# A six-phase Perceiver block on one core: the first phase's prologue taken tile by tile, with its mask, latent values and phase 2's weights moved

## The chip, the cores and the metric

The kernel runs on one core of a Trainium2 chip. The metric is the device time of one execution in microseconds (us); less is better. Times below are of the profiled execution where they carry a place in the trace (us from its start), and of three unprofiled runs where they are called the median.

## What is computed

The reference runs six blocks over x, 64 batches of 32 latent rows with 256 channels (2,048 rows, 16 tiles of 128), with a context of 64 x 257 rows of 192 channels and a mask over the context. The change touches the first block and the entrance of the second:

```
# block 1: cross-attention, 4 heads of 64, per batch
ln   = layernorm(layernorm(x)) * g + b            # 32 latent rows
cn   = layernorm(context) * g + b                 # 257 context rows
q    = rmsnorm(ln @ Wq)
k, v = concat(cn @ Wkv, ln @ Wlkv)                # 257 + 32 keys and values
k    = rmsnorm(k)
x    = x + softmax(masked(q k^T)) v @ Wo + bo     # mask on the 257 context keys
# block 2: self-attention within the 32 rows, 16 heads (16 for q, k and 64 for v)
x    = x + attend(layernorm(x)) @ Wout
# blocks 3 to 6: expert lookup, second cross-attention, state-space scan, routed experts
```

## The kernel before

`layers` (L2719) keeps the rows X in SBUF, 16 tiles of 128 x 256 floats, loads them in four quarters and calls the six phases one behind the other, with a barrier between them. Within a phase every engine has its own program, written by hand, and engines hand over through semaphores. There is no planner; the order of the code is the order of each engine. The helper `skewed(eng, n, depth, step)` (L244) lays a software pipeline over n items: at position v an engine treats item v, item v - 1 and so on, each at its own lag, the first six or so positions unrolled, the middle in a loop of two, the rest unrolled. U = 2 is the number of buffers of most tiles.

Phase 1 has three parts.

**Prologue (`phase1`, L278 to L551).** SP (the DMA queue's engine) issues the loads in order: the last context row of each batch, its vectors, wkv, then wq, wlkv, later weights, and the mask, broadcast to 128 partitions by one DMA (L365). DVE takes the statistics of all 16 tiles of X (L110, L113), normalises all of them into `lat` (L506), takes the statistics of `lat`, and normalises again tile by tile into `ln` (L532). GpSimd (POOL) raises variances to the power -0.5 (L386, L396). Ahead of the tiles stand small steps: PE multiplies the bias and the column sums of the context weights (L405, L408), DVE corrects `wc` (L514, L516), and the 257th context row of all 64 batches is normalised, projected (L417) and turned into the key column 0 of KE and the value row 0 of V3 (L421, L463, L367). Then a pipeline of 16 tiles: PE transposes `ln` (L432), ACT copies it scaled (L471), PE projects q, k and v (L438, L440), ACT squares q and k and copies v to `vl` (L476 to L479), DVE sums and scales (L539 to L547), PE transposes q and k (L446), DVE writes QT (L551) and ACT writes KE (L484). SP copies every `vl` in four DMAs, one a batch, into V3 in SBUF (L373). At the end ACT turns the whole mask from 'keep' to 'drop' (L489).

**Attention (`phase1_attention`, L561 to L776).** A pipeline over 64 batches with depth 4: SP loads two forms of the batch's context, rows (L610) and transposed (L612); DVE takes the rows' statistics (L765); PE multiplies keys and values (L677, L690), DVE scales them (L740), PE transposes keys (L684), forms scores (L657), DVE masks them (L747), ACT takes the exponential (L710), PE transposes the shares (L697) and multiplies them with the values (L669). For the 33 latent and last-row values ACT copies V3 into a double buffer `v3` (L712), which PE reads as its third operand.

**Output projection (`project_out`, L118).** PE multiplies tile by tile (L136). DVE first adds the bias bo to all of X (L148), then per tile adds the product (L154) and takes the statistics (L157).

Phase 2 (L783 on) loads its weights w and wo and the head mask itself (L838); its PE, POOL and DVE programs wait for all three. DVE aggregates, POOL raises to the power (L846), DVE sums the head masks (L1015) and normalises the first tile (L1049), PE transposes it (L961).

## Time and profile before

| what | value |
|---|---|
| median of 3 runs | 3019.74 us (3013.08 to 3022.22) |
| the profiled execution | 3020.78 us, its span 3018.9 us |
| PE busy | 2578.7 us, 85% of the span |
| DVE, ACT, POOL busy | 2065.5, 1479.5 and 619.0 us |
| DMA | 126.09 MB, mean 42 GB/s |
| phase 1 and the entrance of phase 2 | 0 to 560 us of the span |

The span runs from the first to the last instruction; the profiled execution's own time is 1.9 us longer. A row of the timeline gives start, length, engine, line, operation, the tiles written and read, the number of merged instructions, and in brackets the idle time before it with what ended it. "Idle before" of an engine that isn't the last to arrive costs nothing. A float32 matmul of the program stands as two records.

### The profile page before, as it was taken

The numbers are of one execution on the slowest core, as the hardware profiler recorded it, in microseconds if no ns is written. First come the engines' busy times: TensorE is split into PE (matmuls) and PEld (weight loads), VectorE is DVE, ScalarE is ACT, GpSimd is POOL, SyncE is SP. The second block draws the span as 40 slices with busy tenths as digits, with TensorE's granted clock in tenths as the row PEclk, the third lists the DMA queues.
The fourth block names the chain that finished last, engine by engine and source line by source line (L and its number), as shares of the span: only waits on it lengthen the run. The fifth ranks groups of instructions, "written<-read, shape, count | busy, mean of one in ns | idle before, by whom it ended". The sixth has DMA issues, their size and how long they took to land. (4 is left out here: it accounts for less than half of the span.)

```text
span 3018.9 us, 79963 instructions
## 1 busy us (share of the span) xinstructions
PE 2578.7 (85%) x29948; PEld 1912.8 (63%) x29949; DVE 2065.5 (68%) x4874; ACT 1479.5 (49%) x4043; POOL 619.0 (21%) x809
## 2 busy tenths in 40 slices
PE   6699999799788999999979999958467777779993
PEld 3488887455567888888855666633233333669992
DVE  6488887577539888888846888855589999532222
ACT  3555554255215555555526888812576864013330
POOL 3355554111000000000002222200222221012224
PEclk8799999899879999999989999979699999779996
DMA  3122221000300000000001111112000001441113
GB/s 95 46 68 63 65 65 40 36 1 0 139 37 2 2 3 2 2 2 2 2 21 46 45 46 49 39 40 105 0 1 1 1 1 56 161 182 36 37 35 94
DMA packets 71164, 126.09 MB, mean 42 GB/s; under 512 B 10176, under 2 KB 51392, under 8 KB 66368
## 3 DMA queue, kind: packets, MB, share of 16 engines
q1 hardware_dynamic: 67568, 114.06, 11.5%
q0 software_dynamic: 3408, 9.31, 1.1%
q8 instruction: 144, 2.36, 0.3%
q14 instruction: 44, 0.36, 0.0%
HBM read 103.48 MB, written 17.69 MB: 40 GB/s over the span
## 5 line engine op out<-in xcount | busy, mean ns | idle before, releaser
L1323 PE MATMUL s_ps<-s3e_xT,s_down 128*128 128x128 f32 x2048 | 256.0, 279 | 1.3 <-issue 1.3
L1323 PEld LDWEIGHTS s_ps<-s3e_xT,s_down 128*128 128x128 f32 x2048 | 244.9, 194 | 15.7 <-issue 10.2
L1334 PE MATMUL s_ps<-s_up,s3e_gh 128*128 128x256 f32 x1024 | 241.9, 380 | 3.6 <-DVE s3e_gh L1492 2.2
L1334 PEld LDWEIGHTS s_ps<-s_up,s3e_gh 128*128 128x128 f32 x1024 | 185.3, 190 | 25.9 <-issue 2.8
L1382 ACT ACTIVATE s3e_gh<-s_ps 128x512 f32<-128x512 f32 x128 | 76.5, 598 | 235.2 <-PE s_ps L1334 211.2
L2643 ACT ACTIVATE s6e_hT<-s_ps,s_b 128x128 f32<-128x128 f32 x312 | 84.7, 382 | 187.4 <-PE s_ps L2616 187.4
L2284 DVE SCALAR_TENSOR_TENSOR s5c_fresh<-s_ps,s5c_state 128x1024 f32<-128x1024 f32 x124 | 151.4, 1221 | 11.7 <-PE s_ps L2238 4.9
L1368 ACT ACTIVATE s3e_apart<-s3e_number,s3e_picksT 128x128 f32<-128x128 f32 x512 | 156.1, 388 | 1.6
L1688 PE MATMUL s_ps<-s4a_wv,s4b_cT 128*128 128x256 f32 (+1 forms) x512 | 152.8, 407 | 4.5 <-DMA s4b_cT<-ctxR 4.5
L2667 DVE TENSOR_TENSOR s6e_y<-s_ps,s_b 128x256 f32<-128x256 f32 x39 | 16.6, 425 | 202.2 <-PE s_ps L2630 202.2
L2616 PEld LDWEIGHTS s_ps<-s6e_xT,s6e_w 128*128 128x128 f32 x1248 | 147.1, 194 | 5.4 <-ACT s6e_xT L2647 3.5
L2616 PE MATMUL s_ps<-s6e_xT,s6e_w 128*128 128x128 f32 x1248 | 147.6, 277 | 2.9 <-ACT s6e_xT L2647 2.9
L677 PE MATMUL p_ps<-s_wc,s1b_cT 96*128 96x256 f32 x512 | 128.3, 394 | 19.8 <-DMA s1b_cT<-ctxT 19.8
L1691 PE MATMUL s_ps<-s4b_cT,s4a_wk 128*128 128x257 f32 (+1 forms) x512 | 144.6, 412 | 0.0
L2630 PE MATMUL s_ps<-s_w,s6e_hT 128*128 x624 | 141.2, 379 | 0.8 <-DVE s6e_y L2667 0.8
L2290 DVE TENSOR_TENSOR s5c_fresh<-s5c_fresh,s_ps 128x2048 f32<-128x2048 f32 x62 | 141.2, 2277 | 0.0
L1742 ACT ACTIVATE s4b_pr<-s4b_sc,s4b_nm 128x257 f32<-128x257 f32 x256 | 127.7, 502 | 27.3 <-DVE s4b_nm L1791 26.9
L192 POOL MEMSET s4q_half<- 128x1 f32 x1 | 0.1, 98 | 676.9 <-POOLq L2738 676.9
L2089 ACT ACTIVATE s5c_decay<-s5b_dt,s_rate 128x128 f32<-128x128 f32 x384 | 113.8, 388 | 46.1 <-PE s_ps L2238 44.3
L1295 PEld LDWEIGHTS s_ps<-s3e_col_hot,s3e_row_hot 128*32 128x32 f32 x8192 | 117.5, 110 | 27.6 <-issue 27.4
L1295 PE MATMUL s_ps<-s3e_col_hot,s3e_row_hot 128*32 128x64 f32 x8192 | 127.9, 220 | 0.8 <-issue 0.5
L2630 PEld LDWEIGHTS s_ps<-s_w,s6e_hT 128*128 128x128 f32 x624 | 115.5, 190 | 15.3 <-issue 1.2
(428 smaller groups left out, 6309.9 us busy)
## 6 DMA issues: line engine op xcount, KB each, us to landing
s4b_cT<-ctxR SPq DMA_DIRECT2D x64, 257.0 KB, 2.6
s_w<-p_w SPq DMA_DIRECT2D x16, 1024.0 KB, 13.0
s1b_cx<-ctx SPq DMA_DIRECT2D x64, 192.0 KB, 2.7
s1b_cT<-ctxT SPq DMA_DIRECT2D x64, 192.0 KB, 2.9
s_results<-s6e_y SPq DMA_DIRECT2D x39, 128.0 KB
s_down<-p_down SPq DMA_DIRECT2D x1, 4096.0 KB, 22.8
s_up<-p_up SPq DMA_DIRECT2D x1, 4096.0 KB, 32.0
s_silu_z<-s5p_sz SPq DMA_DIRECT2D x4, 1024.0 KB, 5.0
```

The lines of the kernel that those rows point to most:

```text
L677: mm = pe.matmul(banks[:, K_BANK + c.u, j * D:(j + 1) * D], lhsT=cT[:, c.u, k, tok(j)], rhs=wc[:, k, 0:D], start=k == 0, stop=k == 1)
L1295: mm = pe.matmul(banks[cs, bank, at:at + M], lhsT=row_hot[:, i % 2, j, cs], rhs=col_hot[:, i % 2, j, :], start=True, stop=True)
L1323: mm = pe.matmul(banks[:, H_BANK + i % 2, tok(e)], lhsT=down[:, k, i * CH + e, :], rhs=xT[:, c.u, k, :], start=k == 0, stop=k == KT - 1)
L1334: mm = pe.matmul(banks[:, Y_BANK, 0:D], lhsT=gh[:, o.u, e, :], rhs=up[:, e, :], start=e == 0, stop=e == NE - 1)
L1368: ins = act.activation(apart[:, j, :], number[:], ACT.Abs, bias=picksT[:, t.u, 0, q:q + 1], scale=-1.0)
L1688: return pe.matmul(banks[:, V_BANK, j * D:(j + 1) * D], lhsT=cT[rows, d.u, k, tok(j)], rhs=wv[rows, k, :], start=j == k, stop=j != k)
L1691: return pe.matmul(banks[:, K_BANK + m, 0:CTX], lhsT=wk[rows, k, tok(m)], rhs=cT[rows, d.u, k, :], start=k == 0, stop=k == 1)
L1742: ins = act.activation(pr[:, e.u, n, :], sc[:, e.u, n, :], ACT.Exp, bias=nm[:, e.u, n:n + 1], scale=-1.0, accum_out=sums[:, bass.ds(e.b, 1 ...
L2284: dve.scalar_tensor_tensor(part_of(fresh, h, part, 2), banks[:, D_BANK:D_BANK + 2, :].rearrange("p j d -> p (j d)"), floor, part_of(state, ...
L2290: dve.tensor_tensor(part_of(fresh, h, 0, HG), part_of(fresh, h, 0, HG), banks[:, I_BANK:I_BANK + HG, :].rearrange("p j d -> p (j d)"), ALU ...
L2616: mm = pe.matmul(banks[:, H_BANK + 2 * m.u + f // 4, tok(f % 4)], lhsT=w[:, m.u, k, tok(f)], rhs=xT[:, m.u, k, :], start=k == 0, stop=k == ...
L2630: mm = pe.matmul(banks[:, Y_BANK, 0:D], lhsT=hT[:, o.u, f, :], rhs=w2[:, bass.ds(e, 1), f, :], start=f == 0, stop=f == FT - 1)
```

## The change

- Only x's first quarter and the identity matrix are loaded ahead of phase 1; the other quarters are issued within it, between the weights, which are reordered: wq and wlkv come first.
- `skewed` takes a function `beside(v)`, called ahead of position v outside the loop. The small steps that stood ahead of the tiles are spread over the positions of the pipeline with it. `lat` and the second statistics are gone: the variance of both normalisations is formed at once from the first (`var * (1 + eps) + eps^2`), per quarter of x, and `ln` is read from X.
- POOL adds bo to each tile of X in the pipeline; the output projection gets no bias.
- The mask is loaded once (64 x 257 bytes), turned by ACT, stored to memory (`dropped`) and read back broadcast, four batches a tile.
- The latent values are stored per tile to memory (`v3d`) by one DMA; the last row's values by a DMA from ACT's queue. In the attention SP loads 33 rows per batch from there into `v3`; ACT's copy goes.
- The first two batches' context is loaded at the prologue's end, into buffers that now outlive it.
- Phase 2's w and wo are loaded in sixteenths beside the mask pieces, from a class `Second`.

Where the small steps go: on PE the bias row stands at position 3, the column sums at 4, the context row's transposes at 6, its projection at 16 and its key column at 20. On DVE the statistics of the four quarters stand at positions 0, 3, 4 and 5, the context weights and row statistics at 2, the row's normalisation at 3, the bias copy and the correction of `wc` at 5, the row's sums at 17 and its key at 19.

The core of the diff:

```diff
+def skewed(eng, n, depth, step, link=None, links=0, beside=None):
     def lone(v):
+        if beside:
+            beside(v)
         step(lambda s: Item(0, v - s) if 0 <= v - s < n else None)
...
             def _(sp):
-                for dst, src in ((cvec, "p1_cvec"), (wkv, "p1_wkv"), (vec, "p1_vec"), (wq, "p1_wq"), (wlkv, "p1_wlkv")):
-                    sp.dma_start(dst[:], I[src]).then_inc(load, 16)
-                sp.dma_start(mask8[:, :, 0:CTX], I["mask_BxS2_bk0"].unsqueeze(0).broadcast_to([P, B, CTX])).then_inc(load_late, 16)
-                sp.dma_start(V3[0:1, :, :], cv[:]).then_inc(cv_loaded, 16)
-                    for b in range(BT):
-                        sp.dma_start(V3[1:S + 1, c.b * BT + b, :], vl[b * S:b * S + S, c.u, :]).then_inc(v3_loaded[c.u], 16)
+                for dst, src in ((vec, "p1_vec"), (wq, "p1_wq"), (wlkv, "p1_wlkv")):
+                    sp.dma_start(dst[:], I[src]).then_inc(load_p, 16)
+                rows(1)
...
+                rows(2)
+                rows(3)
+                sp.dma_start(kept[:], I["mask_BxS2_bk0"]).then_inc(load_m, 16)
...
+                def beside(v):
+                    if v == 1:
+                        sp.wait_ge(mask_turned, 1)
+                        sp.dma_start(dropped, kept[:]).then_inc(mask_stored, 16)
+                        sp.wait_ge(mask_stored, 16)
+                        sp.wait_ge(mask_zeroed, 1)
+                    if v == NT:
+                        for c in (Item(0, 0), Item(0, 1)):
+                            load_context(sp, c)
+                            load_turned(sp, c)
                 def step(item):
+                    c, m = item(0), item(1)
+                    if c:
+                        sp.wait_ge(vl_ready, c.b + 1)
+                        sp.dma_start(v3d[bass.ts(c.b, BT), 1:S + 1, :], vl[:, c.u, :]).then_inc(v3_stored[c.u], 16)
+                    if m:
+                        sp.dma_start(mask8[:, bass.ts(m.b, BT), 0:CTX], dropped[bass.ts(m.b, BT), :].unsqueeze(0).broadcast_to([P, BT, CTX])).then_inc(mask_loaded, 16)
+                        g.second.load(sp, I, m.b)
...
             def _(pool):
+                def beside(v):
+                    if v == 0:
+                        deviations(0)
+                        pool.wait_ge(load_bo, 16)
+                    if v == 3:
+                        pool.wait_ge(cstat_ready, 1)
+                        pool.tensor_tensor(crs[:], cve[:], half[0:B, :], ALU.pow).then_inc(crstd_ready, 1)
+                        deviations(1)
...
+                        pool.wait_ge(ln_ready, c.b + 1)
+                        pool.tensor_tensor(X[:, c.b, :], X[:, c.b, :], bo[:], ALU.add)
...
             def _(act):
-                act.wait_ge(load_late, 16 * 4)
-                act.activation(mask8[:, :, 0:CTX], mask8[:, :, 0:CTX], ACT.Copy, bias=1.0, scale=-1.0)
+                    if v == 3:
+                        act.wait_ge(load_m, 16)
+                        act.activation(kept[:], kept[:], ACT.Copy, bias=1.0, scale=-1.0).then_inc(mask_turned, 1)
+                    if v == NT:
+                        act.dma_start(v3d[:, 0, :], cv[:]).then_inc(cv_stored, 16)
...
             def _(dve):
-                for t in range(NT):
-                    ins = dve.tensor_scalar(lat[:, t, :], X[:, t, :], mv[:, t, 0:1], rstd[:, t:t + 1], ALU.subtract, ALU.mult)
-                row_stats(dve, link, stats, mv, var, LN_EPS, lat).then_inc(stat_ready, 1)
+                def spread(i):
+                    dve.wait_ge(g.x_loaded[i], 16)
+                    for t in range(i * XC, (i + 1) * XC):
+                        last = dve.bn_stats(stats[:, t, :], X[:, t, :])
...
+                    dve.tensor_scalar(var[:, cs], mv[:, cs, 1], 1.0 + LN_EPS, LN_EPS * LN_EPS, ALU.mult, ALU.add).then_inc(stat_ready, 1)
...
-        project_out(nc, g, "s1o", banks, OT, wo, bo)
+        project_out(nc, g, "s1o", banks, OT, wo)
...
+                c, a = item(0), item(LAG_AT)
+                if a:
+                    after(sp, pv, a.b - 1)
+                    sp.dma_start(v3[0:S + 1, a.u, :], v3d[bass.ds(a.b, 1), :, :].rearrange("b s d -> (b s) d")).then_inc(v3_loaded[a.u], 16)
-                    pe.wait_ge(v3_ready, o.b + 1)
+                    pe.wait_ge(v3_loaded[o.u], 16 * (o.turn + 1))
-                    act.activation(v3[0:S + 1, a.u, :], V3[:, a.b, :], ACT.Copy).then_inc(v3_ready, 1)
...
-            for dst, src in ((w, "p2_w"), (wo, "p2_wo"), (headmask, "headmask8")):
-                sp.dma_start(dst[:], I[src]).then_inc(load, 16)
-            sp.wait_ge(load, 16 * NLOAD)
...
+    def load(self, sp, inputs, t):
+        cols = bass.ts(t, 1536 // NT)
+        sp.dma_start(self.w[:, :, cols], inputs["p2_w"][:, :, cols]).then_inc(self.loaded, 16)
+        sp.dma_start(self.wo[:].rearrange("p v (h d) -> p (v h) d", h=2)[:, bass.ds(t, 1), :],
+                     inputs["p2_wo"].rearrange("p v (h d) -> p (v h) d", h=2)[:, bass.ds(t, 1), :]).then_inc(self.loaded, 16)
```

## Rows read from the trace of the kernel before

**Rows 1.** Busy time by stretch: length, then each engine, granted clock, DMA share, GB/s
```profile
43.60:101.00 57.40, 51.33 (x200) 30.93 (x200) 37.85 (x106) 30.57 (x99) 24.61 (x15) 0.97 0.15 36
...
120.00:500.00 380.00, 377.86 (x4547) 304.93 (x4548) 305.31 (x924) 203.90 (x605) 210.17 (x309) 0.99 0.23 65
```

**Rows 2.** Timeline up to the first tile's second normalisation
```profile
3.53 3.96 POOL L382 MEMSET s_mask<- 128x4624 uint32 x1
...
5.46 4.02 DVE L110 BATCH_NORM_STATS2 p1a_stats<-x_rows 128x6 f32<-128x256 f32 x12 [5.31 <-DMA x_rows<-x]
...
11.34 1.17 DVE L113 BATCH_NORM_AGGREGATE p1a_mv<-p1a_stats 128x2 f32<-128x6 f32 x16
...
12.87 2.94 POOL L386 TENSOR_TENSOR p1a_rstd<-p1a_var,s_half 128x16 f32<-128x16 f32 x1 [5.38 <-DVE p1a_var L115]
...
21.84 1.28 ACT L455 ACT_TABLE_LOAD   x1 [21.68 <-PE p_ps L413]
...
32.37 0.72 DVE L532 TENSOR_SCALAR p1a_ln<-p1a_lat,p1a_mv,p1a_rstd 128x256 f32<-128x256 f32 x2
```

**Rows 3.** Timeline of PE and POOL in the tile pipeline, seventh to sixteenth tile
```profile
54.59 0.38 PE L432 MATMUL p_ps<-x_ident,p1a_ln 128*128 128x128 f32 x2
...
81.16 1.88 PE L440 MATMUL p_ps<-s_wlkv,p1a_lnT 128*128 128x512 f32 x4
...
87.18 0.41 PE L432 MATMUL p_ps<-x_ident,p1a_ln 128*128 128x128 f32 x2
...
77.71 1.63 POOL L396 TENSOR_TENSOR p1a_rn<-p1a_ss,s_half 128x8 f32<-128x8 f32 x1 [1.93 <-DVE p1a_ss L547]
```

**Rows 4.** Timeline of ACT at the prologue's end
```profile
94.56 0.39 ACT L479 ACTIVATE p1a_vl<-p_ps 128x256 f32<-128x256 f32 x1
...
101.39 0.62 ACT L484 ACTIVATE s_KE<-p_ps,s_vec 128x128 f32<-128x128 f32 x2 [1.98 <-DVE s_QT L551]
101.90 13.94 ACT L489 ACTIVATE s_mask<-s_mask 128x16448 uint8<-128x16448 uint8 x1
```

**Rows 5.** DMAs: V's issue durations (ns), L612's landing, the mask's size and landing (us)
```profile
L373 SPq DMA_DIRECT2D s_V<-p1a_vl x64: 527/530/837, 41.1 to 97.1; - x64
...
DMA to landing us min/median/max: 2.8/2.9/3.9
...
s_mask<-mask_BxS_bk SPq DMA_DIRECT2D x1, 2056.0 KB, 16.7
```

**Rows 6.** Timeline at the start of the attention block
```profile
116.10 0.31 POOL L617 MEMSET s1b_pT<- 128x256 f32 x1 [18.80 <-POOLq L314]
...
120.49 3.78 PE L677 MATMUL p_ps<-s_wc,s1b_cT 96*128 96x256 f32 x8 [19.84 <-DMA s1b_cT<-ctxT]
...
124.31 0.88 DVE L740 SCALAR_TENSOR_TENSOR s1b_kn<-p_ps,s1b_crs,s_bias 128x256 f32<-128x256 f32 x2 [4.76 <-PE p_ps L677]
```

**Rows 7.** Attention: groups of ACT and POOL (120 to 510 us), timeline of SP and PE
```profile
L712 ACT ACTIVATE s1b_v<-s_V 33x256 f32 (+1 forms) x62 | 24.8, 400 | 0.0
...
L629 POOL TENSOR_TENSOR s1b_qb<-s_QT,s_headmask 128x256 f32<-128x256 f32 x63 | 38.8, 615 | 60.1 <-DVE s1b_kn L751 60.1
...
132.40 0.59 SPq L612 DMA_DIRECT2D s1b_cT<-ctxT  x1
...
139.76 0.25 PE L669 MATMUL p_ps<-s1b_pT,s1b_v 128*32 128x32 f32 x8
```

**Rows 8.** Output projection: timeline of DVE and PE, and one stretch as in rows 1
```profile
522.12 4.42 DVE L148 TENSOR_TENSOR x_rows<-x_rows,s_bo 128x4096 f32<-128x4096 f32 x1 [3.33 <-PEq L571]
...
522.12 16.49 PE L136 MATMUL p_ps<-s_wo,s_OT 128*128 128x256 f32 x64 [0.60 <-PEq L571]
...
524.00:526.00 2.00, 2.00 (x6) 1.64 (x5) 2.00 (x1) 0.00 (x0) 0.00 (x0) 0.50 0.00 0
```

**Rows 9.** Timeline at the start of phase 2
```profile
542.47 2.90 POOL L846 TENSOR_TENSOR s_rstd<-s_var,s_half 128x16 f32<-128x16 f32 x1 [1.47 <-DVE s_var L115]
...
550.30 0.16 DVE L1015 TENSOR_REDUCE s_fourmask<-s_headmask 128x4 f32<-128x8 f32 x1 [7.98 <-DMA s_headmask<-headmask]
```

More of the change, by code:

```diff
@@ L253, in skewed @@
         lone(v)
+    if beside and lead != lead + 2 * ((n - lead) // 2):
+        beside(lead)
     trips = (n - lead) // 2
@@ L263, in skewed @@
         lone(v)
+    if beside:
+        beside(n + depth)
 def straight(n, depth, step):
@@ L316, in sa @@
                 return actx.enter_context(nc.sbuf_tensor("p1a_" + name, shape, dt))
+            wq = sa("wq", [P, KT, D])
+            wlkv = sa("wlkv", [P, KT, 2 * D])
+            wkv = sa("wkv", [DH, 2, 2 * D])
+            cvec = sa("cvec", [DH, 2, 2])
+            bo = sa("bo", [P, D])
+            kept = sa("kept", [B, CTX], U8)
             stats = sa("stats", [P, NT, 6])
@@ L321, in phase1 @@
             rstd = sa("rstd", [P, NT])
-            lat = sa("lat", [P, NT, D])
             ln = sa("ln", [P, U, D])
@@ new lines, in _ @@
+                g.second.start(sp, I)
+                def beside(v):
[8 more added lines that the diff above has]
+                            load_turned(sp, c)
@@ L379, in _ @@
+                skewed(sp, NT, 2, step, beside=beside)
+                sp.wait_ge(cv_stored, 16)
+                for q in v3_stored:
+                    sp.wait_ge(q, 16 * NT // U)
+                sp.wait_ge(mask_loaded, 16 * NT)
+                sp.wait_ge(load_late, 16 * 2)
             @block.gpsimd
@@ L390, in _, with step @@
+                def step(item):
+                    c = item(2)
+                    if c:
+                        pool.wait_ge(ss_ready, c.b + 1)
+                        pool.tensor_tensor(rn[:, c.u, :], ss[:, c.u, :], bc(half[:], P, 8), ALU.pow).then_inc(rn_ready, 1)
+                        pool.wait_ge(ln_ready, c.b + 1)
+                        pool.tensor_tensor(X[:, c.b, :], X[:, c.b, :], bo[:], ALU.add)
+                skewed(pool, NT, 4, step, beside=beside)
                 pool.wait_ge(css_ready, 1)
@@ L447, in step @@
                         mm.then_inc(qk_tr, 1)
-                skewed(pe, NT, 4, step)
+                skewed(pe, NT, 4, step, beside=beside)
             @block.scalar
             def _(act):
-                act.wait_ge(load, 16 * NLOAD)
-                act.wait_ge(c_tr, 1)
-                for k in range(2):
-                    ins = act.activation(cT[:, k, :], ps[0:DH, 0, 0, k * B:(k + 1) * B], ACT.Identity,
-                                         bias=cvec[:, 1, k:k + 1], scale=cvec[:, 0, k:k + 1])
@@ L606, in _ @@
         def _(sp):
+            sp.wait_ge(zeroed, 2)
             def step(item):
-                c = item(0)
-                after(sp, cmv_ready, c.b - 1)
-                sp.dma_start(cx[:, c.u, :, :], I["ctx_768"][c.b, 0:2 * P, :].rearrange("(j p) c -> p j c", p=P)).then_inc(cx_loaded[c.u], 16)
-                after(sp, values, c.b - 1)
-                sp.dma_start(cT[:, c.u, :, :], I["ctxT"][c.b, :, :, 0:2 * P]).then_inc(c_loaded[c.u], 16)
-            skewed(sp, B, 0, step)
+                c, a = item(0), item(LAG_AT)
+                if c and not (isinstance(c.b, int) and c.b < U):
+                    after(sp, cmv_ready, c.b - 1)
+                    v["load_context"](sp, c)
+                    after(sp, values, c.b - 1)
+                    v["load_turned"](sp, c)
+                if a:
+                    after(sp, pv, a.b - 1)
+                    sp.dma_start(v3[0:S + 1, a.u, :], v3d[bass.ds(a.b, 1), :, :].rearrange("b s d -> (b s) d")).then_inc(v3_loaded[a.u], 16)
+            skewed(sp, B, 3, step)
         @block.gpsimd
@@ L794, in phase2 @@
         banks = s.psum()
-        w = sb("w", [P, KT, QKV])
-        wo = sb("wo", [P, VT, D])
-        headmask = sb("headmask", [P, HK])
+        w, wo, headmask, load = g.second.w, g.second.wo, g.second.headmask, g.second.loaded
         fourmask = sb("fourmask", [P, R4])
@@ L2738, in layers @@
             nc.all_engine_barrier()
+        with ExitStack() as ahead:
+            g.second = Second(Scope(nc, ahead, "s2w"))
+            for phase in (phase1, phase2):
+                run(phase)
+        for phase in (phase3, phase4, phase5, phase6):
+            run(phase)
 def layout(a):
```

264 lines of the change are left out of this document (151 added, 113 removed).

## The prediction

> **What bounds the kernel now.** I read the stage windows first, then the timeline of each engine through the first 135 us, the waits, and then the two places after the attention loop that the diff touches. From 120 to 500 us TensorE (PE) is busy 377.86 of 380.00 us at a granted clock of 0.99: the attention loop is PE-bound and nothing taken from ScalarE (ACT) or VectorE (DVE) shortens it [rows 1]. What can be gained lies before and after it. Before it, the prologue has four serial stretches: statistics and a full normalisation of all 16 tiles up to 32.37 us, in which PE only works on small things [rows 2]; the tiles, 3.6 us each, at which PE is busy 51.33 of 57.40 us [rows 1, 3]; the mask turned by one ACT instruction of 13.94 us with nothing beside it [rows 4]; and the start of the attention block at 116.10, whose first transposed context is used at 120.49 [rows 6]. After it come the bias add of 4.42 us and the wait for phase 2's weights [rows 8, 9].
>
> **First tile earlier.** Only the first quarter of x is issued before the first barrier, three issues fewer, so phase 1's block begins at about 3.1 instead of 3.5. The first quarter is used at 5.46 now [rows 2]; I keep 5.4. Its statistics: 4 x 0.335 (4.02 / 12), 4 x 0.07 for the aggregates (16 of them take 1.17), 0.2 for the variance, and three hand-overs of some 0.05: 2.0, so 7.4. POOL's clearing of the mask (3.96 us from the block's start) ends then too. The power over 16 columns takes 2.94 and over 8 columns 1.63 [rows 2, 3], 0.16 a column, so 1.0 for 4: 8.4. The first normalised tile starts at about 8.9 instead of 32.37, 23.5 earlier. The pass into `lat` and the second statistics go; they are inside this 23.5. The weights wq and wlkv stand in the queue behind 0.6 MB instead of 2.6 MB and come at 7 to 8, by my reading no wait.
>
> **What the fill gives back.** Between the first tile and step 7 of the pipeline the old kernel needed 22.2 us (32.37 to 54.59, the seventh tile's transposes) [rows 2, 3]. The new one has three more things there. ACT's table load, 1.28 [rows 2], now sits between the first transposes and the second, since both use one bank: 1.3. PE gets two pairs of 512-column products (bias row and column sums), 1.88 a pair as in the tile loop [rows 3]: 3.8. DVE gets 9.9: context weights 0.9, context row 0.7, three spreads of statistics at 2.0, 0.4, bias copy and weight correction 2.0. Walking the steps in order, PE is busy with cold first projections and the extra products until about 31, and DVE's normalisation of the sixth tile ends at about 33, behind QT, bias, correction and last spread: 2.3 of the 9.9 show. Together 7.4, of which some 1.4 falls in gaps that the old fill had. Given back: 6.0. Bounds: nothing of DVE's work shows (gives back 3.7), or all does (15). I take the walk, since DVE idled over half of the old fill. Net shift at step 7: 17.5.
>
> **The tiles.** From 54.59 to 87.18 nine steps take 32.6, 3.62 each, PE-bound [rows 3]; I leave them. POOL gets x + bo per tile. The nearest row is qb, 128 x 256 from two SBUF inputs, 0.615 [rows 7]; beside its 1.63 it makes 2.25 of 3.62, behind the power it shall not delay. Price zero, covered by POOL's idle 2.0 per step; if the cover were gone it would add to rn, on which DVE waits. SP has four issues a step as now: one latent store for four, and one mask piece and two weight pieces. Now each takes 0.53 to 0.84 [rows 5], with some 0.15 between, so 2.7 a step. The new ones have more dimensions; at 0.6 to 0.7 each they take 2.9 of 3.62: covered. The latent store is used again two steps (7.2 us) later; landings are 2.9 (a batch of transposed context) to 16.7 (the whole mask of 2 MB, which shares the engines with the other loads) [rows 5], a sixteenth of it much less. Before them SP waits for the turned mask (64 x 257 bytes: about 0.4 on ACT), stores it and waits for it, some 3 us after ACT's step 3, when the second tile's values aren't yet there: zero.
>
> **The tail.** The context row's projection on PE in step 16 costs 1.9. The row's key column costs 0.6 behind the last KE, which ended at 102.01 [rows 4]. So ACT ends at 102.0 - 17.5 + 1.9 + 0.6 = 87.0; square sums and powers of that row lie in DVE's drain idle of 2 us. SP: the last value is copied at 94.95 - 17.5 + 1.9 = 79.4 [rows 4]; behind it come a store, three pieces, four context loads, three pieces: 11 issues at 0.6 = 86.0, landing 2.9 later, 88.9. SP is last. The 13.94 of the mask is gone, with the 0.26 of the barrier kept: the attention block starts at 89.1 instead of 116.10. **27.0 gained.**
>
> **First context.** Now from block start to the first kn is 8.2 us (116.10 to 124.31), because loads are issued inside the block. With both tiles loaded, PE starts keys at once, cold, 3.78 [rows 6], and DVE's statistics with POOL's power (about 2.1) lie beside: 4.0. **4.2 gained**; at full clock the keys would take 1.9, the other bound is 6.1.
>
> **Attention loop.** ACT loses the V copy, 62 x 0.400 = 24.8 [rows 7]. The cover is PE: worth zero, apart from a few tenths in the drain. SP gets a third DMA per item: V for item 0 would be issued behind the transposed context at 133.0 and is used at 139.76 [rows 7], 6.7 us of slack against a landing of 2.9 [rows 5]. Zero, and decided by that slack.
>
> **Output projection.** The 4.42 add on DVE looks like a gain and is none: PE starts at the same 522.12 at clock 0.50 until past 526, DVE catches up, and PE ends the stage: 16.49 busy, without gaps [rows 8]. Between 0 and 4.4; I take 0, since what ends the stage is PE's last product at 538.6 with one add and one statistic behind it.
>
> **Phase 2.** DVE waits 7.98 us for the masks, until 550.30; the power, which would then be last, ended at 545.37 [rows 9]. With everything there, DVE goes on at 545.4. **4.9 gained.** The clock after it is cold either way.
>
> **Sum.** 27.0 + 4.2 + 4.9 = 36.1. The profiled execution took 3020.78 us (span 3018.9), 1.04 above the median of 3019.74. 3020.78 - 36.1 = 2984.7; I say 2984.
>
> **Two rules against it.** The piecewise loads: the rows show four issues per step fitting in 2.7 to 2.9 of 3.62. The Trainium skill, "DMA: Bandwidth & Descriptors", section on rules for kernel authors, says to coalesce small transfers, which below 64 KB are mostly overhead; these are 64 to 128 KB, and by it the queue would set the pace. With the rows the sum has nothing for it, by the rule it has rival B's 5 us; no row of before shows such a piece.
> The add on POOL: no row has a two-input POOL operation beside DVE's normalisation. The Trainium skill, "SBUF — State Buffer", section "SBUF: two separate sides", says that DVE and GpSimd share one port pair as an exclusive lock, held for a whole instruction, where DVE runs a 2-port mode or reads two SBUF tensors; here DVE's operations read one tensor, at 0.405 for 256 columns, so by it they'd pass, and the sum stays. Were the lock taken all the same, it is rival C, priced from rows.
>
> **Rivals.**
> A. The fill is serial: most of DVE's 9.9 shows (7.6 more). For: DVE is in order, and its spreads stand ahead of the normalisation that PE waits for. Against: its idle there. Gain 28.5, time 2992; chance 0.15.
> B. SP sets the tile's pace. At its longest issue (0.84 + 0.15, four a step = 3.96) 14 steps lose 5: gain 31, 2990. Chance 0.07. It would also need the latent store to hold back ACT.
> C. POOL's add blocks DVE or delays rn: 16 x 0.62 = 9.9: gain 26, 2995. Chance 0.05.
> D. The bias add was on the path: 4.4 more, 2980. Chance 0.06.
> E. Slower: V from memory comes late in the attention loop. Place: PE's V product of each item; price: landing less 6.7 us, times 64. At a landing of 7.1 the gain falls below 9 us, at 7.4 the kernel is slower by over 0.3%; 8 us would cost 83 and give 3068. Against: no context landing is over 3.9. Chance 0.03 slower, 0.03 about equal.
> F. A part doesn't do what it says: phase 2 or the first context still waits for something not seen (the clearing of a buffer, a weight piece last in the queue). 4 to 5 less, 2989. Chance 0.05.
> The forecast itself, gains of 31 to 41: 0.56.
>
> **The numbers.** A difference of 0.3% (9 us) is about what a measurement of this kernel can tell from no change. The range reaches to A and C on one side, with the runs' own spread (3013 to 3022), and on the other takes in full clock at the first keys (1.9), D (4.4) and a fill without DVE (2.3): 2972 to 2997. Faster 0.93, within 0.3% 0.04, slower 0.03.
>
> **What the profile after would show.** First `ln` near 9 us; seventh tile's transposes near 37; steps of 3.6; no 13.9 us ACT row; attention's memsets near 89, with the keys at once and first kn 4 us later; the same 6.0 us per item; output projection still 16.5 us of PE; no DMA wait at the start of phase 2. Wrong would be: steps over 3.7 us with SP never waiting (B) or rn late (C), PE idle over 3 us around steps 4 to 6 (A), a wait of PE for V in attention (E), attention starting more than 3 us from 89.

## The result, and the profile after

The changed kernel takes 2987.71 us (median of 4 runs, 2986.72 to 2989.41), the kernel before beside it 3020.82 (4 runs, 3013.08 to 3022.22): a ratio of 0.9896, 95% interval 0.9878 to 0.9914. The profiled execution took 2988.56 us, its span 2986.7. Span against span the gain is 32.2 us, where the prediction's sum said 36.1. A later profiled execution of the same kernel, beside edit 9, stood at 773.03 at the start of phase 3, where this one stood at 772.93, and had a span of 2984.2: behind that place two executions of one program differ by 2.6 us.

The two stretches of [rows 1], the windows of the changed kernel:

```profile
43.60:101.00 57.40, 45.42 (x171) 27.02 (x169) 32.14 (x96) 24.66 (x79) 30.96 (x32) 0.91 0.53 115
120.00:500.00 380.00, 373.60 (x4620) 300.67 (x4619) 301.47 (x907) 187.26 (x552) 203.46 (x300) 0.99 0.24 65
```

At the same clock times these cover other work: the first now holds the end of the tiles and the start of the attention, the second ends behind the attention. So the places have to be followed one by one. First the fill, which answers to [rows 2, 3], from the timelines of POOL, DVE and PE:

```profile
3.22 3.96 POOL L421 MEMSET s_mask<- 128x4624 uint32 x1
5.13 1.41 DVE L569 BATCH_NORM_STATS2 p1a_stats<-x_rows 128x6 f32<-128x256 f32 x4 [4.99 <-DMA x_rows<-x]
7.48 1.05 POOL L427 TENSOR_TENSOR p1a_rstd<-p1a_var,s_half 128x4 f32<-128x4 f32 x1 [0.30 <-DVE p1a_var L574]
8.56 0.73 DVE L620 TENSOR_SCALAR p1a_ln<-x_rows,p1a_mv,p1a_rstd 128x256 f32<-128x256 f32 x2 [1.36 <-POOL p1a_rstd L427]
```
```profile
28.89 1.88 PE L501 MATMUL p_ps<-p1a_wlkv,p1a_lnT 128*128 128x512 f32 x4
...
33.30 0.43 PE L493 MATMUL p_ps<-x_ident,p1a_ln 128*128 128x128 f32 x2 [1.84 <-DVE p1a_ln L620]
33.88 1.69 PE L499 MATMUL p_ps<-p1a_wq,p1a_lnT 128*128 128x256 f32 x4
35.35 3.06 PE L501 MATMUL p_ps<-p1a_wlkv,p1a_lnT 128*128 128x512 f32 x4
...
38.69 0.38 PE L493 MATMUL p_ps<-x_ident,p1a_ln 128*128 128x128 f32 x2
...
73.64 0.44 PE L493 MATMUL p_ps<-x_ident,p1a_ln 128*128 128x128 f32 x2
```

The first tile starts at 8.56 instead of 32.37. PE waits 1.84 for the sixth tile's normalisation, and the product behind that gap takes 3.06 where the one before it took 1.88 (the granted clock is 0.57 from 34 to 38 us). The seventh tile's transposes stand at 38.69, the sixteenth's at 73.64, with the context row's 1.93 between.

The tail and the attention's start, which answer to [rows 4 to 6], from the timelines of ACT, SP, POOL, PE and DVE:

```profile
80.26 0.39 ACT L550 ACTIVATE p1a_vl<-p_ps 128x256 f32<-128x256 f32 x1
...
87.28 0.62 ACT L555 ACTIVATE s_KE<-p_ps,s_vec 128x128 f32<-128x128 f32 x2 [1.95 <-DVE s_QT L639]
87.80 0.58 ACT L535 ACTIVATE s_KE<-p_ps,s_vec 128x64 f32<-128x64 f32 x2
```
```profile
80.84 0.60 SPq L407 DMA_DIRECT2D s_v<-p1a_vl  x1
81.64 0.41 SPq L409 DMA_DIRECT2D s_mask<-s_dropped  x1
...
83.75 0.40 SPq L317 DMA_DIRECT2D s_bcx<-ctx  x1
...
86.22 0.60 SPq L409 DMA_DIRECT2D s_mask<-s_dropped  x1
86.86 0.61 SPq L2814 DMA_DIRECT2D s2w_w<-p_w  x1
87.52 0.60 SPq L2815 DMA_DIRECT2D s2w_wo<-p_wo  x1
```
SP's waits between 80 and 93 us:
```profile
SPq L415 <- DMA s_mask<-s_dropped: 3.0, 1, 3.0
```
```profile
92.06 0.31 POOL L709 MEMSET s1b_pT<- 128x256 f32 x1 [7.10 <-POOLq L322]
...
92.10 3.75 PE L769 MATMUL p_ps<-s_wc,s_bcT 96*128 96x256 f32 x8 [5.15 <-PEq L322]
...
95.89 0.88 DVE L830 SCALAR_TENSOR_TENSOR s1b_kn<-p_ps,s1b_crs,s_bias 128x256 f32<-128x256 f32 x2 [2.88 <-PE p_ps L769]
```

The 13.94 of the mask is gone. ACT is done at 88.38. SP issues until 88.12 and then waits 3.0 for the last mask piece, issued at 86.22 and landed 4.9 later, so SP ends the stage. The two weight pieces behind it are waited for only in phase 2. The keys start 0.04 behind the block.

Behind the attention, which answers to [rows 8, 9], from the timelines of PE, POOL and DVE:

```profile
492.83 16.86 PE L136 MATMUL p_ps<-s_wo,s_OT 128*128 128x256 f32 x64 [0.58 <-PEq L660]
...
513.60 2.89 POOL L928 TENSOR_TENSOR s_rstd<-s_var,s_half 128x16 f32<-128x16 f32 x1 [1.47 <-DVE s_var L115]
...
516.53 0.16 DVE L1097 TENSOR_REDUCE s_fourmask<-s2w_headmask 128x4 f32<-128x8 f32 x1 [3.08 <-POOL s_rstd L928]
```

DVE waited 7.98 for a DMA there; it now waits 3.08 for the power. Where the time went, from the starts of the same instructions (us; the last column is the running gain):

| place | before | after | gain so far |
|---|---|---|---|
| first `ln` | 32.37 | 8.56 | 23.8 |
| seventh tile's transposes | 54.59 | 38.69 | 15.9 |
| sixteenth tile's transposes | 87.18 | 73.64 | 13.5 |
| attention block | 116.10 | 92.06 | 24.0 |
| first `kn` | 124.31 | 95.89 | 28.4 |
| output projection | 522.12 | 492.83 | 29.3 |
| DVE's head-mask sum in phase 2 | 550.30 | 516.53 | 33.8 |
| start of phase 3 | 804.30 | 772.93 | 31.4 |
| span | 3018.9 | 2986.7 | 32.2 |

### The profile page after: what moved, and what is told of

The parts are those of the page before. It is cut to its first block and busy times, and to the rows that moved or that the text cites. A ratio compares the mean times of both kernels' runs of the same rounds, so it can differ in the third digit from the quotient of the medians.

```text
span 2986.7 us, 80073 instructions
## 1 busy us (share of the span) xinstructions
PE 2578.9 (86%) x29948; PEld 1912.3 (64%) x29949; DVE 2050.2 (69%) x4827; ACT 1447.7 (48%) x3979; POOL 628.6 (21%) x827
## 5 line engine op out<-in xcount | busy, mean ns | idle before, releaser
L2749 DVE TENSOR_TENSOR s6e_y<-s_ps,s_b 128x256 f32<-128x256 f32 x39 | 16.6, 424 | 200.8 <-PE s_ps L2712 200.8
L769 PE MATMUL p_ps<-s_wc,s_bcT 96*128 96x256 f32 x512 | 128.1, 394 | 5.2 <-PEq L322 5.2
```

What stands on the lines that cost most here:

```text
L769: mm = pe.matmul(banks[:, K_BANK + c.u, j * D:(j + 1) * D], lhsT=cT[:, c.u, k, tok(j)], rhs=wc[:, k, 0:D], start=k == 0, stop=k == 1)
```

## The experiments

Eleven variants ran, and the changed kernel once more. Where a single time stands the kernel ran once, and it is compared with the profiled changed kernel by its places in the trace; where there were several runs, medians and intervals stand. The totals of single runs decide little: in edits 4 and 8 the seventh tile starts 2.6 and 2.8 us earlier than after the change, in code that those edits leave alone (see the fill, below).

**1. The bias add alone.** The kernel before, with `bo` left out (the output then lacks it):

```diff
-        project_out(nc, g, "s1o", banks, OT, wo, bo)
+        project_out(nc, g, "s1o", banks, OT, wo)
```

> The kernel before, with the add of bo to X left out of the output projection. If PE ends that stage, the stretch from its first product to the next phase's aggregates (522.12 to 540.94 before) keeps its 18.8 us within 0.5 and the kernel its time. If the bias add was on the path, it shrinks by 4.4 us.

Measured 3017.59 us beside 3022.39. PE's 64 products took 15.54 instead of 16.49 and started at 520.81; from their start to DVE's aggregates in phase 2 there were 17.87 us instead of 18.82. The 0.95 between the two is PE's own duration, that is the clock; behind the change itself the same stretch is 19.24, with the add gone. The 4.42 us row was hidden, and rival D falls. The total alone would have pointed the other way, 4.8 below the run beside it; but runs of the kernel before range from 3013.08 to 3024.2, and at the start of phase 3 the two stand at 804.23 and 804.30.

**2. The context loads back inside the attention.** The loads at position 16 go, the attention's SP issues them; its wait for the cleared buffers moves behind them, to the first load of V.

```diff
@@ prologue, sync
-                    if v == NT:
-                        for c in (Item(0, 0), Item(0, 1)):
-                            load_context(sp, c)
-                            load_turned(sp, c)
@@ attention, sync
-                if c and not (isinstance(c.b, int) and c.b < U):
+                if c:
```

> The kernel after, with the first two batches' context loaded inside the attention block again. The first kn comes 8.2 us after the block's start instead of 3.8 (+4.4). But SP has four issues fewer at the prologue's end: if SP's queue is what ends the prologue, the block starts 2 us earlier than 92.06, and the first kn stands at 98.3, net +2.4. If ACT ends the prologue, the block's start stays and the net is +4.4.

Measured 2989.05. From block to first `kn` 8.04 us instead of 3.83, as expected (before 8.2). But the block came at 88.85, 0.26 behind ACT's last write of KE, 3.2 us earlier than after the change. The net is 1.0 later at the first `kn` (96.89), 0.5 later than in the changed kernel's other profile (96.38). So the four issues ahead of the last mask piece in SP's queue cost 3.2 of the 4.2 that they bring, and they hold the end of the prologue. By the total, 2989.05 against 2985.78 to 2989.41 of the changed kernel, the early loads are worth nothing that can be told.

**3. Phase 2's weights loaded whole in phase 2, as before the change.**

```diff
-                        g.second.load(sp, I, m.b)
+            for dst, src in ((w, "p2_w"), (wo, "p2_wo")):
+                sp.dma_start(dst[:], I[src]).then_inc(load, 16)
```

> The kernel after, with w and wo of phase 2 loaded in phase 2 again, one DMA each. First normalisation of phase 2 moves from 4.5 to about 9.4 us behind the phase's first aggregate (+4.8). SP issues two DMAs fewer per tile: if SP ends the prologue, the attention block starts 2 to 2.5 us earlier than 92.06, net +2.5; steps of the tile pipeline stay 3.65 us if neither SP nor the small rows cost anything there, and fall to 3.61 if they did.

Measured 2990.32. The tiles' step stayed at 3.67 us (34.96 from the seventh to the sixteenth tile, less the context row's 1.93, over nine steps), without the two weight pieces a step as with them (before 3.62), which removes rival B: the pieces cost the tiles nothing. The block came at 89.98, 2.1 earlier. Only 0.9 of that is SP's shorter tail (from ACT's last KE to the block 2.76 instead of 3.68); the other 1.2 stood already at the sixteenth tile (72.46 instead of 73.64). The last mask piece was issued 2.5 earlier, at 83.74, but SP waited 5.1 for it. The wait came back, in DVE's timeline:

```profile
517.07 0.16 DVE L1101 TENSOR_REDUCE s_fourmask<-s2w_headmask 128x4 f32<-128x8 f32 x1 [7.55 <-DMA s2w_wo<-p_wo]
```

4.5 lost at phase 2's entrance, 0.9 gained in the tail.

**4. The mask turned whole at the end again**, by the long ACT instruction.

```diff
-                        act.activation(kept[:], kept[:], ACT.Copy, bias=1.0, scale=-1.0).then_inc(mask_turned, 1)
+                        act.activation(kept[:], kept[:], ACT.Copy).then_inc(mask_turned, 1)
...
+                act.wait_ge(mask_loaded, 16 * NT)
+                act.activation(mask8[:, :, 0:CTX], mask8[:, :, 0:CTX], ACT.Copy, bias=1.0, scale=-1.0)
```

> The kernel after, with the mask stored unturned and turned in the 128-partition copy at the prologue's end, as in the kernel before. The turning needs the last piece, which lands at about 91, so it stands fully behind SP: attention starts at 92.06 + 13.9 = 106 us. If the pieces' landing were not what ends the prologue, ACT would turn from 88.4 on and attention start at 102.6 (+10.5).

Measured 2996.61. The timeline of ACT:

```profile
85.24 0.58 ACT L535 ACTIVATE s_KE<-p_ps,s_vec 128x64 f32<-128x64 f32 x2
88.21 13.95 ACT L560 ACTIVATE s_mask<-s_mask 128x16448 uint8<-128x16448 uint8 x1 [2.40 <-DMA s_mask<-s_dropped]
```

From ACT's last KE to the block there are 16.6 us instead of 3.7: 12.9 for 13.95 of instruction, since ACT had idled there behind SP. It is the largest single part of the gain behind the fill. The block's place, 102.42, looks like the second figure of the expectation (102.6, if the landing didn't count); it isn't that case, since the trace shows ACT waiting 2.40 for the last piece. ACT's last KE simply ended 2.6 earlier, at 85.82. For the same reason the total rose by 8.9 only.

**5. DVE's small work out of the fill.** The bias copy goes to ACT at position 4, the correction of `wc` to DVE's position 16.

```diff
@@ vector
-                    if v == 5:
-                        dve.tensor_copy(bias[:], banks[:, B_BANK, :]).then_inc(bias_ready, 1)
+                    if v == NT:
                         for k in range(2):
                             ins = dve.scalar_tensor_tensor(wc[:, k, :], ...)
@@ scalar
+                    if v == 4:
+                        act.activation(bias[:], banks[:, B_BANK, :], ACT.Copy).then_inc(bias_ready, 1)
```

> The kernel after, with DVE's correction of wc moved from position 5 to 16 and the bias copy given to ACT at position 4. DVE reaches the sixth tile 2 us earlier, so PE's wait of 1.84 us at 31.5 goes. If that wait is also what let the clock fall (the next products took 3.06 instead of 1.88 and 1.69 instead of 1.03), the seventh tile's transposes move from 38.69 to about 35.0 (3.6 to 3.7 gained). If the wait alone counts: 36.8.

Measured 3005.28, 17.6 us slower than the change. The first half went as expected: PE's 1.84 gap was gone, the granted clock from 34 to 38 us was 1.00 (0.57 after the change), and the seventh tile's transposes stood at 35.31 instead of 38.69. Here the wait and the slow products behind it went together: from the fifth tile's transposes to the seventh's 8.27 us instead of 11.49, that is 3.2, of which the gap is 1.8 and the clock 1.4. Edits 4 and 8 show that they aren't one cost: there the same gap stood at the same place, 1.83, the products behind it took 1.13 and 1.88, and from the sixth tile to the seventh there were 3.97 and 3.98 us instead of 5.39. Then two losses that no theory had. PE at position 16 needs `wc` before DVE, a position behind, has corrected it (timeline of PE; first row with the wait, whose products are slow again):

```profile
71.71 3.65 PE L479 MATMUL p_ps<-p1a_wkv,p1a_cT 96*64 96x512 f32 x4 [3.26 <-DVE s_wc L606]
75.28 0.69 PE L493 MATMUL p_ps<-x_ident,p1a_ln 128*128 128x128 f32 x2
```

5.0 lost. And phase 3, which this kernel entered 1.1 us ahead of the changed one (771.83 against 772.93), was longer by 17.0 us from its normalisation at 876.3 (876.9 after the change) to the last one (541.9 instead of 524.9), in code that the edit doesn't touch. DVE's waits there, 1080 to 1400 us (waiter, what it waited for, us in total, times, longest), and PE's from 1050 to 1500:

```profile
DVE s3e_xn L170 <- issue: 16.7, 4, 4.3
```
```profile
PE s_ps L1396 <- DVE s3e_xn L170: 8.9, 4, 2.4
```

"Issue" is time in which DVE waited for nothing that the profile shows. In the changed kernel it has none in this loop.

**6. SP's tail shortened.** The whole mask by one DMA at position 1, phase 2's weights in four parts within the attention, the context loads at position 4.

```diff
+                        sp.dma_start(mask8[:, :, 0:CTX], dropped.unsqueeze(0).broadcast_to([P, B, CTX])).then_inc(mask_loaded, 16)
-                    if v == NT:
+                    if v == 4:
                         for c in (Item(0, 0), Item(0, 1)):
...
-                    if m:
-                        sp.dma_start(mask8[:, bass.ts(m.b, BT), 0:CTX], ...)
-                        g.second.load(sp, I, m.b)
@@ attention, sync
+                if 2 <= v < 6:
+                    g.second.load(sp, I, v - 2)
```

> The kernel after, with the mask read back in one DMA once it is stored, the first context loads issued at position 4, and phase 2's weights loaded in quarters at the start of the attention. SP's last issue in the prologue is the last latent store (80.8, landed by 85), so ACT's last write at 88.4 ends it: attention starts at 88.7 instead of 92.06, 3.4 gained. If something else than SP's queue held it, the start stays at 92. The weights cost the attention nothing if a transposed context still lands within its 6 us of slack; otherwise PE waits for it in the first steps.

Measured 2982.73. ACT's last KE ends at 88.71 and the block starts at 88.97: SP no longer ends the stage, 3.1 us gained at the first `kn` (92.80), and 2.9 of it still there at the start of phase 3.

**7. V from memory loaded one position later**, where it is used at once.

```diff
-                c, a = item(0), item(LAG_AT)
+                c, a = item(0), item(LAG_OUT)
...
-            skewed(sp, B, 3, step)
+            skewed(sp, B, 4, step)
```

> The kernel after, with each batch's V rows loaded one step later, so that the slack of 6.6 us is gone (about 0.6 us left). PE then waits for V in every item: landing of 2.5 to 3 us less 0.6, so 2 to 3 us for each of 64 items, 130 to 190 us in all. If the loop hid it (V not on PE's path) the time would stay.

Measured 3172.59, 184 us more, 2.9 an item. PE's waits between 100 and 600 us, and that kernel's window against [rows 1]:

```profile
PE p_ps L761 <- DMA s1b_v<-s_v: 104.5, 53, 2.3
```
```profile
120.00:500.00 380.00, 297.51 (x3138) 236.28 (x3137) 206.28 (x621) 131.43 (x374) 141.69 (x208) 0.88 0.18 47
```

Each item waits up to 2.3, and PE's clock falls with the gaps (0.88 granted). Rival E's place is right, and what keeps it away is the one position of slack. Its price is too low: by its formula an item costs what it waits, 2.3 at most, and here it cost 2.9, the rest being products at the lower clock.

**8. ACT's copy kept**, as a dummy copy of as many elements per item in the attention.

> The kernel after, with a copy of 33 x 256 values put back into ACT's step of the attention where the V copy stood (to a buffer nobody reads). 64 x 0.4 = 25.6 us of ACT's busy time come back. If PE bounds the loop, an item stays at 6.07 us and the time is the same within 1 us; if ACT's order counted, up to 25 us more.

Measured 2986.02. The groups of ACT in that attention:

```profile
L804 ACT ACTIVATE s1b_spare<-s_bias 33x256 f32<-33x256 f32 x63 | 25.2, 400 | 0.0
```

25.2 us of work came back. The total, 2.5 below the profiled changed kernel's, isn't the proof of that, since the first `kn` stood 2.8 earlier, at 93.07, by the clock in the fill. The stage is: from first `kn` to the output projection 397.8 us before, 396.9 after the change, 397.8 here. The 24.8 of the old copy were worth at most 0.9, and less than can be told: without the copy the same stretch took from 396.1 (edit 11) to 398.2 (edit 9).

**9 and 10. Fill and tail together, beside the changed kernel itself.** The correction of `wc` at DVE's position 6, the bias copy left where it is, and the whole of edit 6; and the changed kernel unaltered.

```diff
@@ vector, from position 5 to position 6
+                    if v == 6:
+                        dve.wait_ge(rstd_ready, 4)
                         for k in range(2):
                             ins = dve.scalar_tensor_tensor(wc[:, k, :], ...)
```

> Moves DVE's correction of wc (two of 0.63 us) from position 5 of the tiles to position 6, where DVE had 1.0 us of idle time, and makes the whole of the change to SP's tail that the earlier kernel made (mask copied with one DMA, second phase's weights in four parts instead of 16, context loads at position 4). DVE issues as many instructions as in the changed kernel. My theory (the DVE-caused PE gap of 1.84 us and the cold clock behind it are one cost of 3.4 us; SP's tail is another of 3.1 us, and they add): PE's wait for ln(5) falls to about 0.6 us, its next products run at 1.88 us or at most half of the 1.2 us excess stays, T(6) at 35.9 to 36.5, the block at 86.0 to 86.8 by ACT, span 2978 to 2980, a ratio to the kernel before of 0.986 to 0.988. Rival (the DVE work only moves its wait to position 6 and costs there what it saved): T(6) at 38 or more or T(7) - T(6) at 5, total as with the tail alone, 2983. Rival (a loss in the third phase, as when DVE lost one instruction): +17 us there, total 2996.

> The changed kernel unaltered, as the measure for the run beside it: 2987 to 2990 us, ratio 0.989 to 0.990 to the kernel before. In its third phase DVE waits for no instruction (issue idle 0).

The combination took 2983.57 (4 runs, 2981.11 to 2984.71), ratio 0.9881 (0.9865 to 0.9897); the changed kernel 2986.07 (2985.78 to 2987.51), ratio 0.9893 (0.9877 to 0.991). The figure of the first rival (38 or more) holds for the fill, though for another reason than it gives, and the theory of the expectation missed the seventh tile, the block (88.20) and the total. PE's wait for `ln`(5) fell to 0.64 and its products stayed at 1.88, but the next step was late. The timeline of ACT:

```profile
35.85 0.38 ACT L548 ACTIVATE p1a_vl<-p_ps 128x256 f32<-128x256 f32 x1 [4.66 <-DMA s_v<-p1a_vl]
```

ACT can't reuse `vl` because its store stands in the queue behind the mask's one transfer of 2056 KB, issued at 21.95. The kernel of edit 6 has the same 4.66, at 36.37; there it fell beside PE's slow products and cost nothing (from the sixth tile's transposes to the seventh's 5.40, after the change 5.39). Here they stand at 38.16. The mask in sixteen pieces was not needed for its own sake, but it keeps the stores of V moving.

**11. The bias copy alone moved to ACT.** Nothing else differs from the changed kernel.

```diff
@@ vector, position 5
-                        dve.wait_ge(b_summed, 1)
-                        dve.tensor_copy(bias[:], banks[:, B_BANK, :]).then_inc(bias_ready, 1)
@@ scalar, position 4
+                        act.wait_ge(b_summed, 1)
+                        act.activation(bias[:], banks[:, B_BANK, :], ACT.Copy).then_inc(bias_ready, 1)
```

> The changed kernel with the bias copy alone moved from DVE (position 5) to ACT (position 4), so that DVE's program is one instruction shorter and all else on it stands in the same order. Theory of the 17 us that the third phase lost when the copy went to ACT: it is DVE's instruction supply in that phase's loop, which depends on where DVE's code lies, so the loss comes back here: DVE waits for issue some 4 times 4.2 us ahead of its normalisation, phase 3's loop about 17 us longer, total some 3004 us. Rival (it was the moved correction of wc, or an accident of that one execution): no such waits, total 2986 to 2989. The prologue: PE's wait for ln(5) 1.84 - 0.68 = 1.2 us, T(6) earlier by 0.7 us, by 2.5 if the clock then holds.

Measured 3002.26, 16.2 above the changed kernel's median on the same chip. The waits of DVE in phase 3's loop:

```profile
DVE s3e_xn L170 <- issue: 17.4, 4, 4.6
```

So the loss of phase 3 has nothing to do with the correction of `wc` (nor with ACT's added copy, which edit 12 keeps). It comes with a DVE program that is shorter ahead of the loop by the copy and the wait before it. In the prologue the same kernel gained: PE's gap was 1.24, its next products ran at 1.88, and the seventh tile's transposes stood at 36.56, 2.1 before the unaltered kernel's 38.67.

**12. All of it together.** The copy on ACT and, in its old place on DVE, a copy of a single column; the second phase's weights in four parts at SP's positions 0 to 3, the context loads at position 4, the mask in its 16 pieces.

```diff
-                        dve.tensor_copy(bias[:], banks[:, B_BANK, :]).then_inc(bias_ready, 1)
+                        dve.tensor_copy(spare[:], wkv[:, 0, 0:1])
```

> The changed kernel with (1) the bias copy made by ACT at position 4, and in its old place on DVE a copy of one column (some 0.1 us), so that DVE's program is as long as in the changed kernel; (2) the second phase's weights loaded in four parts of 640 KB at SP's positions 0 to 3; (3) the first context loads at SP's position 4; the mask stays in 16 pieces, one per tile. Theory of the third phase's loss (it goes with the length of DVE's program ahead of that loop, which the two kernels that lost it had one instruction shorter): no issue idle on DVE there and the 17 us stay away. Theory that the whole mask's one transfer of 2056 KB held back the stores of V in the kernel with both edits (ACT waited 4.66 us for one): with the mask in pieces that wait is gone or under 1 us, PE's wait for ln(5) is 1.2 us with its next products at 1.88 us, T(6) at 36.3 to 36.9, the last column of KE ends at 86.0 to 86.7, the block at 86.3 to 87.0, first kn at 90.1 to 90.9. Total 2979 to 2981 us, ratio 0.986 to 0.988. Rival on the third phase (the copy's place on ACT or an accident of code): 2996. Rival on the transfers (640 KB parts or the context loads hold back a store as the mask did): ACT waits 2 to 5 us for a store and T(6) or T(7) is later by as much, total 2982 to 2985.

Measured 2980.52 (4 runs, 2978.22 to 2984.48), ratio 0.9867 (0.985 to 0.9883), against 0.9893 (0.9877 to 0.991) of the unaltered change: better by its median, with intervals that still overlap. DVE has no issue wait in phase 3's loop, so filling the place of one instruction brings back the 16 us that edit 11 lost. ACT has no wait for a store. The block came at 87.85, 0.25 behind ACT's last KE, 4.7 before the unaltered kernel's 92.55 in the run beside edit 9. The total was met, but the places from the seventh tile on were missed, all by about 1 us. The timeline of PE:

```profile
30.82 0.31 PE L475 MATMUL p_ps<-x_ident,p1a_cn 64*96 64x64 f32 x2
32.44 0.43 PE L495 MATMUL p_ps<-x_ident,p1a_ln 128*128 128x128 f32 x2 [1.30 <-DVE p1a_ln L625]
33.02 1.39 PE L501 MATMUL p_ps<-p1a_wq,p1a_lnT 128*128 128x256 f32 x4
34.20 3.36 PE L503 MATMUL p_ps<-p1a_wlkv,p1a_lnT 128*128 128x512 f32 x4
```

Behind a gap of 1.30 the clock fell here; behind the 1.24 of edit 11 it held. The gap's length doesn't decide that, for behind the 1.83 of edits 4 and 8 it held too. The seventh tile's transposes stand at 37.83 instead of 36.3 to 36.9, the block at 87.85 instead of 86.3 to 87.0, the first `kn` at 91.69 instead of 90.1 to 90.9. Over edit 6 this execution gained 1.1 up to the first `kn` and 5.7 up to phase 3. Most of the difference is clock: the output projection's products took 15.44 instead of 17.01, and phase 2 from its first tile's transposes to the fourth's 40.54 instead of 43.58. So not all of the 2980.52 is owed to the edits.

## Why the prediction was right, and where its terms were off

The total was forecast 2984 with a range of 2972 to 2997 and came at 2987.7. What the change gains, and where, held step by step; the sizes of two terms were off, the tail's and the fill's, and part of the fill's miss is the clock of one execution.

- **First tile**: 8.9 forecast, 8.56 measured, with the power over 4 columns at 1.05 (1.0).
- **Fill**: 6.0 given back by the sum, 7.9 measured (23.8 less 15.9). The DVE-caused wait was right in place and size (2.3, measured 1.84). Missed was the clock of the products behind it: 1.69 and 3.06 instead of 1.10 and 1.88, with the granted clock at 0.57 in 34 to 38 us, that is 1.2 GHz for most of it. It moves the seventh tile by 1.4. A second piece of clock stands earlier: the second tile's products of 512 columns took 3.39 here and 2.17 in edit 8, and the third tile's transposes stood at 19.16 and 17.77. In edits 4 and 8, which leave the fill's work as it is, both pieces are absent and the fill gave back 5.4 and 5.3. So the forecast of 6.0 lies between what the same work takes at one clock and at the other; that it came near is in part luck. The bound "or all does (15)" left out the 1.4 that falls in old gaps and should read 13.6.
- **Tiles**: 3.62 a step, measured 3.67; the projection of the context row 1.9, measured 1.93. Rivals B and C fall: SP waited for ACT's values 23.6 us over 14 steps, and POOL's add took more than the row it was priced from, 0.734 against 0.615, on nobody's path. By the Trainium skill, "DMA: Bandwidth & Descriptors", section on rules for kernel authors, small transfers are to be coalesced, and those under 64 KB cost mostly overhead; the pieces here, of 64 to 128 KB, lie just above that. The trace agrees in part: they land 3.2 to 4.1 us after their issue (medians), later than the 192 KB of a context in the attention (2.6 and 3.0), though the prologue's own context loads take 3.2 and 4.0 as well. But the four issues fit: 0.60, 0.41, 0.65 and 0.43, with what lies between them 2.7 of a step of 3.67 (80.84 to 83.53), as the prediction had it. And with the mask in one transfer a store of V came late (edit 9).
- **Tail**: 89.1 forecast, 92.06 measured: the term that was off most. ACT's end, forecast at 87.0, came at 88.38, moved by the fill's shift, which was 15.9 where 17.5 was forecast. SP's last issue was forecast at 86.0 and ended at 88.12, since the same miss moved it and 11 issues took 7.3 instead of 6.6. And the sum let SP wait for its last issue with the landing of a context load (2.9); SP waits for the last mask piece, issued two before the last, and that took 4.9. Which wait ends the stage was right, and edits 2 and 6 show it: without the tail the block follows ACT by 0.26.
- **First context**: 4.2 forecast, 4.4 measured. The keys ran cold (3.75, granted clock 0.50 in the stretch), as the sum had it.
- **Attention**: zero forecast for ACT's copy, 0.9 measured at most; V's slack held. PE waited for V in no item, and edit 7 shows that the slack decides it. In rival E the landing of 7.1 at which the gain was to fall below 9 us gives 10.5 by its own formula (64 times 0.4 off 36.1).
- **Output projection**: the bias add worth 0, measured 0 with a difference of 0.4 the other way by PE's clock.
- **Phase 2**: 4.9 forecast, 4.9 measured (9.36 to 4.46 from the aggregates to the head-mask sum). But 2.4 of the gain were lost again in that phase. From its first tile's transposes to the fourth's it took 43.44 us (517.16 to 560.60), 40.78 before (550.93 to 591.71), with a granted clock of 0.50 between 548 and 552. In the kernels of edits 3, 4, 5 and 12 the same stretch took 41.8, 40.9, 40.8 and 40.5, in the others that keep the attention's time 42.9 to 43.6. "The clock after it is cold either way" was right for its start and not for its length. What decides between the two is open: it follows neither the edit nor the total.

Together: block −3.0, first context +0.2, attention +0.9, output projection −0.4, behind phase 2's entrance −1.6, which makes the 36.1 into 32.2. The last three are of the size by which executions of one kernel differ.

## What to carry to other kernels

A gap of PE is priced by its own length, and the products behind it by either clock: the same 1.8 us of waiting cost 3.2 in one execution and 1.8 in others, so a forecast needs both as bounds. Before a single run's total is read, compare the places ahead of the edit: the fill alone moved them by up to 2.8 us here. Where a stage ends at a barrier, what counts is the landing of the last transfer that is waited for there, so put that transfer ahead of those that nobody waits for yet; and don't place one large transfer ahead of small stores that free a buffer. After any edit, compare the phases that it doesn't touch as well: here one instruction less (with its wait) in an engine's program cost 16 us, a thousand lines further on in the code.

## What the runs showed of the hardware that was not expected

- **Instruction supply.** With one DVE instruction fewer ahead of it, and its wait, phase 3's loop shows DVE idle for 4.1 to 4.6 us, "issue", ahead of one instruction, four times in 320 us; PE waits 8.9 and 9.7 us in all for it, and its granted clock falls to 0.98 from 1.00. Both kernels with the program so shortened had it (edits 5 and 11), the changed kernel and those with its full length not, and the one with a filler in the place not either. Shortness isn't the cause by itself: the kernel before, with one DVE instruction taken out of its output projection (edit 1), shows no such wait. The windows of 1080 to 1400 us, edit 11 and then edit 12:

```profile
1080.00:1400.00 320.00, 310.28 (x5372) 271.08 (x5372) 265.22 (x858) 164.41 (x372) 0.00 (x0) 0.98 0.01 3
```
```profile
1080.00:1400.00 320.00, 319.82 (x5589) 279.15 (x5588) 276.20 (x874) 174.04 (x391) 0.00 (x0) 1.00 0.01 2
```

  That it is the place of the loop in DVE's program which decides is what fits these runs; how the instructions are fetched they don't show, and no other lengths were tried.
- **POOL beside DVE.** POOL's add of 128 x 256 takes 0.720 to 0.743 us in all 16 tiles. The row that it was priced from, 0.616 in the attention, is another operation, a product with a mask that is read again for each query, so the difference of 0.12 says nothing on DVE. DVE's normalisations kept their 0.40 for 256 columns. By the Trainium skill, "SBUF — State Buffer", section "SBUF: two separate sides", a DVE operation takes the shared port pair from GpSimd when it runs a 2-port mode or reads two SBUF tensors; the trace agrees in that nothing stood still beside DVE operations that read one.
- **Landings.** With the queue as full as here, a weight piece of 64 KB lands 3.2 us after its issue, one of 96 KB 3.6, a mask piece of 128.5 KB 4.1 (medians; at most 4.5, 3.9 and 4.9): twice the size adds 0.9.
- **Clock behind a gap.** PE's gap ahead of the sixth tile's transposes was 1.83 or 1.84 us in eight profiles of kernels that share the fill. In two of them (edits 4 and 8) the products behind it ran at 1.13 and 1.88, in the other six the clock fell and the stretch from the sixth tile to the seventh was 1.1 to 1.4 longer (5.09 to 5.40 instead of 3.97 and 3.98). So the length of a gap doesn't tell whether the clock falls behind it; what does, these runs leave open.
